# Record scatters divided anew among the stages and paced by marks, in a four-layer graph network on one core

## What is computed

```python
edge_index = stack([src, dst])
x = layernorm(x + L0(x))  # mean of x[dst] over the edges of a src node, then an MLP
x = layernorm(x + L1(x))  # attention: softmax over the edges of each dst node, then an MLP
x = layernorm(x + L2(x))  # (x + 3 * sum of weight * x[dst] over the edges of src) / 4
x = layernorm(x + L3(x))  # messages by edge type, summed at dst and at src
# inside L1, with 4 heads:
alpha = einsum('ehc,ehc->eh', q[dst], k[src] + e) / sqrt(C)
amax = segment_max(alpha, dst, num_segments=n)
ex = exp(alpha - amax[dst])
alpha = ex / (segment_sum(ex, dst)[dst] + 1e-16)
agg = segment_sum((v[src] + e) * alpha, dst)
```

## Time and profile before

| | us |
|---|---|
| runs | 4649.19, 4655.66, 4657.07 |
| median | 4655.66 |
| span of the profiled execution, first to last instruction | 4651.0 |
| PE busy | 2871.3 (62%) |
| DVE busy | 2230.8 (48%) |
| ACT busy | 613.9 (13%) |
| POOL busy | 3414.1 (73%) |

### The profile page before, as it was taken

How to read it: one execution, slowest core, us unless ns; L and a number is a source line. 1 busy time by engine, 2 the same in 40 slices (tenths; PEclk the granted TensorE clock), 3 DMA queues, 4 the chain that set the end, 5 groups by cost and what they waited for, 6 DMA issues and landing times. The chain is left out here.

```text
span 4651.0 us, 50018 instructions
## 1 busy us (share of the span) xinstructions
PE 2871.3 (62%) x13750; PEld 2210.0 (48%) x13751; DVE 2230.8 (48%) x2711; ACT 613.9 (13%) x1076; POOL 3414.1 (73%) x3213
## 2 busy tenths in 40 slices
PE   3799998967777777751989643444444333333333
PEld 1688887943333333331989433333333333333333
DVE  7899997656666666668971621111111111111112
ACT  0355554010000000001751000000000000000000
POOL 1888886857777777767867677777777777777775
PEclk8899999968877878875999866666666566555556
DMA  6466566816666666651989523222222122212221
GB/s 191 139 189 183 170 187 209 265 37 172 170 170 170 170 171 173 173 153 59 278 241 276 174 68 94 68 68 68 68 68 68 49 53 52 53 53 53 53 53 51
DMA packets 498663, 599.91 MB, mean 129 GB/s; under 512 B 190115, under 2 KB 367441, under 8 KB 496248
## 3 DMA queue, kind: packets, MB, share of 16 engines
q0 software_dynamic: 117856, 246.12, 19.4%
q1 hardware_dynamic: 337751, 229.77, 17.7%
q10 hardware_dynamic: 42944, 122.68, 7.3%
HBM read 406.69 MB, written 204.36 MB: 131 GB/s over the span
## 5 line engine op out<-in xcount | busy, mean ns | idle before, releaser
L1151 PE MATMUL ps<-got,g_hot 128*128 x3224 | 719.2, 414 | 1151.3 <-DMA got<-y_back,s_msg 597.5
L721 POOL DMA_INDIRECT rec_by_src<-rec,pos x782 | 1123.9, 1437 | 344.1 <-issue 245.8
L1151 PEld LDWEIGHTS ps<-got,g_hot 128*128 128x128 f32 x3224 | 667.8, 316 | 1213.1 <-issue 1213.1
L1612 POOL DMA_INDIRECT sc_kv<-kv,d_src x806 | 762.0, 945 | 254.9 <-issue 245.3
L1036 POOL DMA_INDIRECT got<-y_forward,d_msg x782 | 739.1, 945 | 238.2 <-issue 238.2
L1036 POOL DMA_INDIRECT got<-y_back,s_msg x766 | 722.7, 943 | 241.7 <-issue 233.1
L806 PE MATMUL ps<-ln_low,ln_hot 128*125 128x256 f32 x2848 | 618.9, 380 | 19.7 <-DVE ln_low L783 15.9
L806 PEld LDWEIGHTS ps<-ln_low,ln_hot 128*125 128x125 f32 x2848 | 535.3, 188 | 103.2 <-issue 22.7
L1059 DVE TENSOR_TENSOR g_hot<-ps,src_loc 128x1024 f32<-128x1024 f32 x101 | 123.4, 1224 | 832.1 <-PE ps L1151 831.7
L1715 PE MATMUL ps<-q,sc_hotT 128*128 x1616 | 274.2, 322 | 236.4 <-DVE sc_hotT L1657 207.4
L1067 DVE TENSOR_TENSOR g_y<-ps,ms_b 128x384 f32<-128x384 f32 x75 | 41.8, 558 | 732.1 <-PE ps L1164 732.1
(11 more groups left out here) (328 smaller groups left out, 3102.4 us busy)
## 6 DMA issues: line engine op xcount, KB each, us to landing
linked<-ln_out SPq DMA_DIRECT2D x320, 224.0 KB
ve<-sc_kve ACTq DMA_DIRECT2D x202, 256.0 KB
wv_ve<-ve SPq DMA_DIRECT2D x101, 512.0 KB, 5.0
l_links<-linked SPq DMA_DIRECT2D x25, 800.0 KB, 7.3
l_links<-linked ACTq DMA_DIRECT2D x25, 800.0 KB, 9.2
attr_pairs<-ln_feats POOLq DMA_DIRECT2D x7, 2048.0 KB
sc_attr<-attr_pairs SPq DMA_DIRECT2D x202, 64.0 KB, 2.6
sc_kv<-kv,d_src POOLq DMA_INDIRECT x806, 3.0
```

The lines of the kernel that those rows point to most:

```text
L721: pool.indirect_dma_start(out=dram["rec_by_src"], out_offset=bass.IndirectOffsetOnAxis(ap=S["pos"][:, c:c + 1], axis=0), in_=S["rec"][:, c ...
L1151: last = pe.matmul(ps[:, bass.ds(columns[j], width)], hot[:, q, j, :], got[:, bass.ds(slots[j], width)], start=False, stop=True, skip_grou ...
L1612: pool.indirect_dma_start(out=kv[:, q, j, :], out_offset=None, in_=dram["kv"], in_offset=bass.IndirectOffsetOnAxis(ap=S["d_src"][:, c:c + ...
```

## The change

The 782 scatters are divided anew. `index_stage` issues ten before its gathers and fourteen behind them. `mlp_layer`, `project` and `norm_and_messages` no longer issue them in one run: POOL waits on counts that PE and DVE keep anyway (`turned`, `hidden`, `product`, `biased`). In `mlp_and_linked_sum` a new semaphore `eased` is counted up by the products 1, 9 and 17 (counted from 0) of each block; four scatters are free and each other one waits for one mark. In `softmax_maxima` the front mark moves to `index_stage` and the loads of the four node lists move to SP's queue in `scores`, before step 24 (of 202); the lists' tiles live through both stages. The division is done with logarithms: ACT takes the log of each sum (with 1e-16 added as its bias), DVE subtracts it from the score, ACT takes the exponential again. The first exponential goes to another tile, so that the scores stay.

Blank lines and most unchanged lines are left out, and so are the declarations of the new tiles and of `eased`.

```diff
@@ -387,7 +387,7 @@
-RECORD_PARTS = {"index": 6, "link": 302, "l0": 70, "m0": 30, "project": 22, "maxima": 82, "weigh": 100, "m1": 42, "l2": 76, "norm": 0}
+RECORD_PARTS = {"index": 24, "link": 312, "l0": 70, "m0": 25, "project": 15, "maxima": 113, "weigh": 106, "second": 79, "norm": 0}
@@ -437,6 +437,9 @@
         below = m.sb(tag + "_below", [P, TILES])
+        front = m.sb(tag + "_front", [1, 1])
+        fronted, begun = m.sem(tag + "_fronted"), m.sem(tag + "_begun")
+        LATER = 14
@@ -462,6 +465,9 @@
             whole = records.rearrange("(t e) r -> t (e r)", e=P)
+            if send is not None:
+                first, last = part_of(send)
+                send_some(pool, S, dram, first, last - LATER)
@@ -469,10 +475,12 @@
             if send is not None:
-                send_records(pool, S, dram, send)
+                send_some(pool, S, dram, last - LATER, last)
         @block.sync
         def _(sp):
+            sp.wait_ge(fronted, 1)
+            sp.dma_start(dram["node"][0:1].rearrange("(a n) -> a n", a=1), front[:, :]).then_inc(begun, 16)
@@ -486,6 +494,7 @@
             sp.wait_ge(filed, 16 * len(stairs))
+            sp.wait_ge(begun, 16)
@@ -532,6 +541,7 @@
+            dve.memset(front[:, :], -1.0).then_inc(fronted, 1)
@@ -1283,7 +1293,14 @@
         def _(pool):
-            send_records(pool, S, dram, tag)
+            sent, last_sent = part_of(tag)
+            each = -(-(last_sent - sent) // CHUNKS)
+            for c in range(CHUNKS):
+                for sem, some in ((turned, each - 2 * (each // 3)), (hidden, each // 3), (product, each // 3)):
+                    pool.wait_ge(sem, c + 1)
+                    pool.nop(nofuse=True)
+                    send_some(pool, S, dram, sent, min(sent + some, last_sent))
+                    sent = min(sent + some, last_sent)
@@ -1334,6 +1351,8 @@
     WAYS, WIDE = 4, 4
+    EASE_AT = (1, 9, 17)
+    EASE = len(EASE_AT)
@@ -1379,8 +1399,13 @@
         def _(pool):
-            send_records(pool, S, dram, "m1")
-            send_records(pool, S, dram, "l2")
+            first, last = part_of("second")
+            free = last - first - BLOCKS * EASE
+            send_some(pool, S, dram, first, first + free)
+            for n in range(BLOCKS * EASE):
+                pool.wait_ge(eased, n + 1)
+                pool.nop(nofuse=True)
+                send_some(pool, S, dram, first + free + n, first + free + n + 1)
@@ -1437,6 +1462,8 @@
                                      start=False, stop=True, skip_group_check=True)
+                    if k in EASE_AT:
+                        last.then_inc(eased, 1)
@@ -1498,7 +1525,11 @@
         def _(pool):
-            send_records(pool, S, dram, "project")
+            first, last = part_of("project")
+            for n in range(last - first):
+                pool.wait_ge(product, max(1, n * BLOCKS // (last - first)))
+                pool.nop(nofuse=True)
+                send_some(pool, S, dram, first + n, first + n + 1)
@@ -1614,8 +1645,13 @@
         def _(sp):
+            rows = P * PAIRS_PAD
             for n in range(STEPS):
                 i, q = divmod(n, WAYS)
+                if n == 4 * WAYS:
+                    for name, a in (("before", dram["node"][0:rows]), ("node", dram["node"][1:1 + rows]), ("after", dram["node"][2:2 + rows]),
+                                    ("place", dram["loc"].rearrange("b e -> (b e)")[0:rows])):
+                        sp.dma_start(S["mx_" + name][:, :], a.rearrange("(p c) -> p c", p=P)).then_inc(S["noded"], 16)
@@ -1757,16 +1790,15 @@
         into = m.sb("mx_into", [P, HEADS])
-        front = m.sb("mx_front", [1, 1])
         turned, kept, stored, loaded, order, asked, told, ready, exped, shared, done = (m.sem("mx_" + n) for n in (
             "turned", "kept", "stored", "loaded", "order", "asked", "told", "ready", "exped", "shared", "done"))
-        fronted, noded = m.sem("mx_fronted"), m.sem("mx_noded")
+        summed, logged, weighted = (m.sem("mx_" + n) for n in ("summed", "logged", "weighted"))
+        guard = m.sb("mx_guard", [P, 1])
         divided, refilled = ([m.sem(f"mx_{n}{h}") for h in range(HEADS)] for n in ("divided", "refilled"))
         ps = S["ps"]
         HALF_T = 14
         block = stack.enter_context(nc.Block())
         flat_alpha = dram["alpha"].rearrange("h b e -> h (b e)")
-        flat_loc = dram["loc"].rearrange("b e -> (b e)")
@@ -1803,7 +1835,13 @@
                 act.wait_ge(ready, h + 1)
-                act.activation(score[:, h, :], score[:, h, :], ACT.Exp).then_inc(exped, 1)
+                act.activation(back[:, h, :], score[:, h, :], ACT.Exp).then_inc(exped, 1)
+            for h in range(HEADS):
+                act.wait_ge(summed, h + 1)
+                act.activation(back[:, h, :], back[:, h, :], ACT.Ln, bias=guard[:, 0:1]).then_inc(logged, 1)
+            for h in range(HEADS):
+                act.wait_ge(weighted, h + 1)
+                act.activation(score[:, h, :], score[:, h, :], ACT.Exp).then_inc(shared, 1)
@@ -1812,17 +1850,11 @@
         def _(sp):
-            sp.wait_ge(fronted, 1)
-            sp.dma_start(dram["node"][0:1].rearrange("(a n) -> a n", a=1), front[:, :]).then_inc(stored, 16)
-            sp.wait_ge(stored, 16)
-            for t, a in ((node_b, dram["node"][0:P * L]), (node, dram["node"][1:1 + P * L]),
-                         (node_a, dram["node"][2:2 + P * L]), (loc, flat_loc[0:P * L])):
-                sp.dma_start(t[:, :], a.rearrange("(p c) -> p c", p=P)).then_inc(noded, 16)
             for h in range(HEADS):
                 sp.wait_ge(kept, (h + 1) * PAIR_BLOCKS)
                 sp.dma_start(dram["alpha"][h].rearrange("(c p) e -> p c e", p=P),
                              turn[:, h * PAIR_BLOCKS:(h + 1) * PAIR_BLOCKS, :]).then_inc(stored, 16)
-            sp.wait_ge(stored, 16 * (1 + HEADS))
+            sp.wait_ge(stored, 16 * HEADS)
@@ -1836,8 +1868,8 @@
             link = Chain(dve, order)
-            dve.memset(front[:, :], -1.0).then_inc(fronted, 1)
-            dve.wait_ge(noded, 16 * 4)
+            dve.wait_ge(S["noded"], 16 * 4)
+            link(dve.memset(guard[:, :], 1e-16))
@@ -1899,7 +1931,7 @@
             dve.wait_ge(exped, HEADS)
-            carried(2, False, same, score, top, 0.0, ALU.mult, ALU.add)
+            carried(2, False, same, back, top, 0.0, ALU.mult, ALU.add)
@@ -1907,10 +1939,11 @@
                 carry(h, open_a, back, ALU.add, ALU.max)
-                link(dve.tensor_scalar_add(back[:, h, :], back[:, h, :], 1e-16))
-                link(dve.reciprocal(back[:, h, :], back[:, h, :]))
-                dve.tensor_tensor(score[:, h, :], score[:, h, :], back[:, h, :], ALU.mult).then_inc(shared, 1)
-            dve.wait_ge(shared, HEADS)
+                dve.engine_nop().then_inc(summed, 1)
+            for h in range(HEADS):
+                dve.wait_ge(logged, h + 1)
+                dve.tensor_tensor(score[:, h, :], score[:, h, :], back[:, h, :], ALU.subtract).then_inc(weighted, 1)
+            dve.wait_ge(weighted, HEADS)
@@ -2103,7 +2136,13 @@
         def _(pool):
-            send_records(pool, S, dram, "norm")
+            first, last = part_of("norm")
+            for n in range(last - first):
+                if n:
+                    pool.wait_ge(biased, n * BLOCKS * PIECES // (last - first))
+                    pool.nop(nofuse=True)
+                send_some(pool, S, dram, first + n, first + n + 1)
+            pool.wait_ge(S["sent"], 16 * TILES)
```

More of the change, by code:

```diff
@@ L1347, in mlp_and_linked_sum @@
         landed = [m.sem(f"f_landed{q}") for q in range(WAYS)]
+        eased = m.sem("f_eased")
         cleared, summed, turned, kept, hidden, active, product, biased, gelued, varied, rooted, order, normed = (
@@ L1744, in softmax_maxima @@
         turn = m.sb("mx_turn", [P, HR, P])
[L1745 to L1748, removed]
+        node, node_b, node_a, loc = (S["mx_" + name] for name in ("node", "before", "after", "place"))
         bad = m.sb("mx_bad", [P, L])
@@ L2286, in gnn_kernel @@
             S["alpha"] = a.sb("alpha_cols", [P, HEADS, PAIR_COLS])
+            for name in ("before", "node", "after", "place"):
+                S["mx_" + name] = a.sb("mx_" + name, [P, PAIRS_PAD])
+            S["noded"] = a.sem("mx_noded")
             with ExitStack() as early:
```

## The result

The changed kernel takes **4712.17 us** (median of four runs, 4709.72 to 4717.25); the kernel before, run beside it, 4654.26 us (4649.19 to 4657.07). The ratio is 1.0129, with a 95% interval of 1.0115 to 1.0143: **1.3% slower**. The forecast was 4705 us, 4672 to 4730.

A forecast was written before the change was run, and what follows sets the result against it. POOL's queue of 782 scatters was taken to close the softmax and index stages. Terms +10, +34, +1, +2, +3 sum to 50 on a span of 4651.0, 4701; with 4.7 added 4705.7, say 4705 us; range 4672 to 4730.

The forecast's parts named there:

- POOL closes the softmax: Softmax stage: POOL's drain ends last, so the some 26 us that DVE and ACT gain don't show.
- The index term: Index stage: eight more scatters behind the gathers, on a queue that already closes the stage, +10 us (8 to 18).
- The spacing under DVE's work: Softmax stage: 48 scatters at 1.70 us beside hindering DVE work, 65 at 1.27 us after it, together 164 us.
- unhindered scatters: Rival, softmax stage: scatters lose nothing under DVE's work, -21 us there, kernel 4685 us; chance 0.08.
- the tail of the drain: Softmax stage's end: 3.1 us where scatters end unhindered, as in the second sum, against 7.6 us before.
- the softmax term: Softmax stage, 82 to 113 scatters: POOL ends at 2230 instead of 2196.3, +34 us (13 to 48).
- The second sum: Second linked sum, 118 to 79 scatters: nothing freed, the last waits for a late mark, +2 us (0 to 6).
- The norm: Norm stage, 52 to 38 scatters paced on DVE's additions: late release, landing and drain, +3 us (0 to 5).
- the data path: Rival, softmax stage: POOL isn't the bound, DVE's and ACT's 26 us show in full, kernel 4646 us; chance 0.08.
- marks that hold nothing: Rival, second sum and norm: POOL lags the marks, their +5 us isn't paid, kernel 4700 us; chance 0.07.
- more hindrance: Rival: softmax scatters stay at 1.54 us with a 7.6 us tail, +14 there, some 6 in index, 4725 us; chance 0.12.
- the cases between: Softmax scatters at 0.9 to 1.2 us each, issue included: kernel within 0.2% of before; chance of same 0.07.

The follow-up runs named there:

- experiment 1: The kernel before with only the new softmax arithmetic, old scatter counts and bursts: 4647.82 us, ratio 0.9999 to the kernel before.
- experiment 3: The kernel before, old arithmetic, with 113 instead of 82 scatters in the softmax and 31 fewer in the second sum: 4689.45 us, ratio 1.0087.
- experiment 2: The changed kernel with its new counts, but scatters in bursts again, without marks: 4702.22 us, ratio 1.0113 to the kernel before.
- experiment 4: The kernel before with the new softmax arithmetic and scatters spread anew in bursts, 61 in the softmax: 4617.99 us, ratio 0.9932.
- experiment 5: The changed kernel with one more POOL drain before the sixth-last scatter of the second sum: 4713.67 us, ratio 1.0139 to the kernel before.
- experiment 7: The changed kernel with one more POOL drain before the 24th-last scatter of the second sum: 4710.97 us, ratio 1.013 to the kernel before.
- experiment 6: The kernel with new softmax arithmetic and 61 softmax scatters, plus a drain behind the 59th of 118 second-sum scatters: 4617.48 us, ratio 0.993.

## Why the prediction was right, and where it was short

**That POOL closes the softmax, and the new arithmetic hides under it**, was right, and experiments 1 and 3 show it from both sides: new arithmetic with old count, no change; old arithmetic with new count, +40 us.

**The index term** (+10) came out at +9.7, with POOL's drain last, as forecast, by 11 us. **Weighing** and **scores** came out as said, **link** at its upper end; POOL now closes the link stage (at 797.05, SP is ready at 795.7) and the weighing stage (at 2450.3, DVE is ready at 2448.0).

**The spacing under DVE's work** was right. Forecast: 48 scatters at 1.70 us and 65 at 1.27, 164 us. Measured: 55 in 91.6 us, which is the forecast's 48 at 1.70 with seven of the others at 1.27 (90.5), and 58 at 1.26; from the first start to the last end 164.5 us. A scan and the scatter that it holds, in the changed kernel's timeline:

```profile
2093.76 1.86 DVE L1901 TENSOR_TENSOR_SCAN mx_top<-mx_before,mx_score 128x816 f32<-128x816 f32 x1
...
2094.88 1.50 POOL L731 DMA_INDIRECT rec_by_src<-rec,pos  x1 [0.30 <-issue]
```

The scan ends at 2095.62 and the scatter at 2096.38, 0.76 us later, as in the earlier trace rows. The Trainium skill's 115 ns (SBUF — State Buffer, A bandwidth-pool intuition that's wrong), on which the rival of unhindered scatters rested, doesn't fit this instruction.

**The step that failed is the tail of the drain.** The forecast took 3.1 us, from the second sum before the change, and put the 7.6 us of the softmax down to hindered scatters. Both readings were wrong. The 3.1 stand behind a burst in which POOL had just stopped behind its 113th scatter, so only five were left, and most of it is their landing: the trace's semaphore events have the last landing at 2565.85, 2.9 us behind the last record, and POOL let go 0.24 us later. The 7.6 stand behind 82 scatters, of which the last landed 4.2 us behind its record; where 82 landed within 1.2 us, in experiment 1, the tail is 6.75. What a drain takes goes by the number of scatters since the last drain or stop. It shows cleanest in the norm stage, where POOL waits first until all have landed: 3.152 us behind 38 scatters in the changed kernel, and 4.295 behind 52 before, 0.083 us each both times. Behind the 113 of the softmax it is 9.28 us from the last scatter's end, behind the 79 of the second sum 6.51, 0.082 each; experiment 3, with old arithmetic and 113, has 9.28 too. The forecast's remark on its 4.0 and 7.6 us suggests data still on its way; in the norm stage all had landed before the drain began, so that is not the whole of a tail. The row that held the price was among those that I quoted; I read its 4.3 us as a fixed cost.

With 0.082 per scatter the softmax term comes right without any other change: 34 - 3.1 + 9.3 = +40.2 (measured 40.2). The second sum comes to 2 - 3.1 + 6.5 = +5.4 (measured 6.7, above the 0 to 6 that the forecast gave it). The norm stays between +2 and +3, and measured 4.7. Most of what is left in these two is how far POOL lagged its last marks. PE's last products and the last scatter of the second sum:

```profile
2613.83 5.75 PE L1463 MATMUL ps<-x_rows,got 128*128 128x128 f32 x50
...
2618.78 0.96 POOL L731 DMA_INDIRECT rec_by_src<-rec,pos  x1 [0.83 <-PE ps L1463]
```

The scatter ended at 2619.73, 1.8 us behind its mark (2613.83 + 18/25 x 5.75 = 2617.97), where I had allowed 1. In the norm stage POOL lagged its marks at the end: its last scatter started at 2699.9, as DVE's last addition ended, 73.4 us into the stage, where I had put its release at 71.9.

**The marks.** That they hold the last scatter to the stage's end was right, and so was that taking 39 scatters from the second sum frees nothing: PE was through 167.7 us into the stage before and 168.0 after. What the sum had too low is what the marks cost: 11.9 us for the two stages by experiment 2, not 5.

**Of the rivals**, the data path is refuted by experiment 1, unhindered scatters by the 1.67 us, marks that hold nothing by experiment 2; "more hindrance" came nearest in its softmax term (+48 against +40), but for another reason than it gave. What the forecast says of the cases between, that 0.9 to 1.2 us a scatter would end within 0.2% of before, is wrong at its upper end: 2062.7 + 113 x 1.2 + 3.1 = 2201.4 is 5 us later than before, and with the 16 us of the other terms the kernel would be 21 us slower, 0.5%. Nothing was measured there.

**The forecast's own signs.** ACT through at 2179, the last scatters alone at 1.26 and the longer index stage came as said. The softmax stage, given as some 168 us, took 175, and the second sum, which was to keep its length within 3 us, got 6.7 longer: both are the tail of the drain, in the second sum with the lag beside it.

**The total.** On the spans the forecast was +50 and the measurement +64.4. Of the 14.4 us between them the softmax's tail has 6.2, the second sum 4.7 and the norm stage 1.7; the rest is spread over stages that differ as much from run to run. By the medians it is +58, and 4712 us stand against 4705.

## What to carry to other kernels

Work that is laid beside a stage is free only until its own queue is later than the stage, and that must include what the queue does behind its last record; so look at where the barrier's drains end, not at the last instruction. A shorter data path in a stage that another queue closes gains nothing until that queue is relieved; here, with the shorter path in place, its 26 us came by a new division of the counts alone (experiment 1 against 4). Pacing a background queue to the end of a stage puts its drain on the path: pace it so that it ends early, or not at all.

## What the runs showed of the hardware

- Where the scatters land within about 1 us, a drain of POOL costs about 0.082 us for each of them since the last drain: 2.2 us behind 25, 5.8 behind the 70 of the first linked sum (in all nine profiles), 6.5 behind 79, 8.7 behind 106, 9.28 behind 113 (the same in five runs with that count). Behind 6 (experiment 5) it is 1.4, of which 1.1 are their landing. So a scatter takes 0.96 + 0.30 us at once and 0.08 later. In the link stage, with other transfers between, it is only 4.23 us behind 302 (kernel before).
- Where landing is late the figure looks different (landing by the trace's semaphore events). In experiment 2 the 79 scatters of the second sum, beside link loads, had landed at 2557.59 and POOL let go at 2560.85, 3.26 us or 0.041 each; behind 55 in experiment 7 it was 2.29 us from the landing (2576.12 to 2578.41), 0.042 each, behind 59 in experiment 6 2.44 (2452.33 to 2454.77), 0.041, and behind the 82 of the softmax before the change 3.38 (2192.90 to 2196.28), 0.041. These fit a drain of two passes of 0.041 us a scatter, of which the second waits for the landing; the passes themselves are worked out, not seen. They would account for the 9.8 us of experiment 6: 7.4 until the landing, 2.4 behind it.
- A burst of 118 scatters has a stop of 8.7 to 9.8 us behind the 113th, in the kernel before and in experiments 1 and 4; 113 x 0.082 is 9.3. With a drain in between it doesn't come. Whether it is due at just 113, why the link stage has none, and what fills up, wasn't tried.
